# Attention scores in PSUM: four banks in turn for the exponentials, three for the maxima, with their products issued singly

## The chip, the cores and the metric

The kernel runs on one core of a Trainium2 chip. The metric is the device time of one execution in microseconds; lower is better. The kernel before has a median of 2086.16 us over three runs (2078.07 to 2087.5). TensorE (PE) multiplies and writes PSUM, VectorE (DVE) and ScalarE (ACT) read PSUM, GpSimd (POOL) works on SBUF, SyncE (SP) issues transfers.

## What is computed

One hybrid block in fp32 on x of shape (4, 1024, 256): attention, a routed feed-forward layer, a Mamba-2 layer, and the same feed-forward layer again, each on a layer norm of x and added to x. Only the attention is touched:

```python
Q, K, V = (split(Q), split(K), split(V))      # 16 heads of 16, from multi-LoRA projections
Q, K = (_rope(Q), _rope(K))
scores = jnp.einsum('bhqd,bhkd->bhqk', Q, K) / jnp.sqrt(jnp.asarray(D_KV, x.dtype))
causal = jnp.tril(jnp.ones((s, s), bool))
scores = jnp.where(causal, scores, jnp.asarray(-jnp.inf, scores.dtype))
attn = jax.nn.softmax(scores, axis=-1)
out = jnp.einsum('bhqk,bhkd->bhqd', attn, V)
out = out.transpose(0, 2, 1, 3).reshape(b, s, D_MODEL)
return _multilora(out, ids, Wo, Ao, Bo)
```

## The kernel before

The scores are computed twice. A first pass only finds the largest score of each row of Q. A second pass computes the scores transposed, with that maximum already subtracted inside the product (an extra row of operands), so that ACT can take the exponential straight from PSUM.

The work is cut into 16 units (`UNITS`: 4 batches by 4 groups of 4 heads). A unit has 24 steps (`CORE`), 384 in all, and two pairs of heads, which alternate. TensorE's program is one list, in this order at each step:

- `shifted(U, n)` (L940 to L951): the second pass. Two products, one for each head of the pair, on rows 0 to 63 and rows 64 to 127 of the array, of 512, 384, 256 or 128 columns. They go to two banks of `a_ps_e`, which has `HEAD_BANKS` banks used in turn. Ahead of the first of the two stands the one wait for both banks: on the semaphore `exp_done` of ACT's exponentials (L947).
- `scores(k)` (L928 to L938): the first pass. Products, called chunks, are numbered k from 0 to 767 (`TOTAL`), and come in pairs k and k+1, again one for each half of the array. On average there is one pair per step, but the table `CUTS` gives some steps none and others two. Each chunk takes a bank of `a_ps_m`.
- pieces: LoRA weights ("lora"), transposes of x ("xt"), projections of Q and K ("qk"), of V ("v") and of the output ("out"), and the transpose of the row maxima ("max"). Each takes one bank of `a_ps_m` as well.
- `weigh_at(N - 4)` (L973): the exponentials of an earlier step times V, into `a_ps_a`.

Chunks and pieces together make one list, `entries`, and entry i uses bank i mod `BANKS` of `a_ps_m`. `bank_of` (L848) waits until entry i minus `BANKS` (`BEFORE`) has been read out: a chunk by its maximum on DVE (`chunk_max`), a "lora" or "out" piece by DVE, the other pieces by ACT. PSUM has 8 banks: `HEAD_BANKS` is 3, `BANKS` is 4, and `a_ps_a` has one.

On the other side, `exponential` (L767) runs two ACT instructions per step (L774), one for each bank of the pair. `maxima` (L505) runs one DVE instruction per chunk: on a chunk that crosses the diagonal, an add of the causal mask with a running maximum (L511, followed by a read of the accumulator), on the others a plain reduction (L515). Between them DVE does layer norms, merges and row statistics. All engines run their own instructions strictly in program order, so a wait at `scores(k)` on TensorE also holds back everything behind it in the list: the weighing, the next `shifted`, and with that ACT.

Of the kernel before, what the change touches and what calls it, by code (L numbers as in the profile page):

```python
# [22 lines left out]
P = 128  # L23
# [90 lines left out]
def attention(nc, X, C, A):  # L114
# [2 lines left out]
    UNITS = BATCH * GROUPS  # L117
    BUFS = 5
    RING = 7
    BANKS = 4  # L120
    HEAD_BANKS = 3
    STEPS = [(c, j) for c in range(2) for j in range(HALF * (c + 1))]
    NS = len(STEPS)
    CORE = 2 * NS
# [11 lines left out]
    def width(k):  # L136
        i, c, _ = CHUNKS[k % NC]
        return min(512, (i + 1) * P - 512 * c)
# [60 lines left out]
    entries += LATE  # L199
    BANK = {e: i % BANKS for i, e in enumerate(entries)}  # L200
    BY_DVE = [e for e in entries if e[0] in ("lora", "out")]
# [7 lines left out]
    SELECT_NO = {e: i for i, e in enumerate(SELECTS)}  # L209
    BEFORE = {e: entries[i - BANKS] for i, e in enumerate(entries) if i >= BANKS}  # L210
    assert len(BANK) == len(entries)

    with ExitStack() as held, ExitStack() as ctx:
        sems = Semaphores(nc, held)

        def sb(name, shape, dt=F32):
            return ctx.enter_context(nc.sbuf_tensor("a_" + name, shape, dt))
# [3 lines left out]

        ps_e = ctx.enter_context(nc.psum_tensor("a_ps_e", [P, HEAD_BANKS, 512], F32))
        ps_m = ctx.enter_context(nc.psum_tensor("a_ps_m", [P, BANKS, 512], F32))
        ps_a = ctx.enter_context(nc.psum_tensor("a_ps_a", [P, 512], F32))
# [31 lines left out]
        q_st = sb("q_st", [P, BUFS, SEQ], F32R)  # L256
# [39 lines left out]
        def rows(r):  # L296
            return slice(64 * r, 64 * r + 64)
# [428 lines left out]
        def _(act):  # L726
# [40 lines left out]
            def exponential(U, n):  # L767
# [4 lines left out]
                for r in range(2):  # L772
                    act.wait_ge(shifted_ps, 2 * N + r + 1)
                    nc.scalar.activation(probs[:, N % RING, r, q0:], ps_e[:, (2 * N + r) % HEAD_BANKS, q0:], ACT.Exp,  # L774
                                         scale=DH ** -0.5).then_inc(exp_done, 1)
# [11 lines left out]
            for m in range(4):  # L787
                act.wait_ge(wt_ps, m + 1)
                nc.scalar.copy(w_t[:, m], ps_e[:, m % HEAD_BANKS, :].rearrange("p (t d) -> p t d", t=DT)).then_inc(wt_sb, 1)
            act.dma_start(rope[:], A["rope"]).then_inc(rope_in, 16)  # L790
            for m in range(4):
                act.wait_ge(wt_ps, 5 + m)
                nc.scalar.copy(b_t[:, m], ps_e[0:64, (4 + m) % HEAD_BANKS, 0:D]).then_inc(wt_sb, 1)
            for e in EARLY:
# [34 lines left out]
        def _(pe):  # L829
            ident = C["ident"]  # L830
            pe.wait_ge(w_in, 16 * 4)
            for m in range(4):
                if m >= HEAD_BANKS:
                    pe.wait_ge(wt_sb, m - HEAD_BANKS + 1)
                for d in range(DT):
# [12 lines left out]
            def bank_of(e):  # L848

                if e in BEFORE:  # L850
                    old = BEFORE[e]
                    if old[0] == "chunk":
                        pe.wait_ge(chunk_max, old[1] + 1)
                    elif old in ACT_NO:
                        pe.wait_ge(piece_act, ACT_NO[old] + 1)
                    else:
                        pe.wait_ge(piece_dve, DVE_NO[old] + 1)
                return ps_m[:, BANK[e]]
# [69 lines left out]
            def scores(k):  # L928

                p, (i, c, _) = k // NC, CHUNKS[k % NC]  # L930
                banks = [bank_of(("chunk", k + r)) for r in range(2)]
                if k % NC == 0:
                    pe.wait_ge(pair_in[p % BUFS], 32 * (p // BUFS + 1))
                w = width(k)
                for r in range(2):
                    nc.tensor.matmul(banks[r][:, 0:w], q_st[rows(r), p % BUFS, i * P:(i + 1) * P],  # L936
                                     k_st[rows(r), p % BUFS, 512 * c:512 * c + w], start=True, stop=True
                                     ).then_inc(score_ps, 1)  # L938

# [53 lines left out]
            for k in range(0, CUTS[0], 2):  # L993
                scores(k)
                if k + 1 in AMID:
                    piece(AMID[k + 1])
            for U in range(UNITS):
                for n in range(CORE):
                    N = U * CORE + n
                    shifted(U, n)  # L1000
                    for k in range(issued_after(N - 1), issued_after(N), 2):
                        scores(k)
                    for e in pieces_after(U, n):
                        piece(e)
                    if N >= 4:
                        weigh_at(N - 4)
                    if N >= 2 and issued_after(N - 2) == TOTAL:
                        keep_warm()
# [1336 lines left out]
def phase_attention(nc, X, C, I, out):  # L2345
    A = {k: I["L0_attn_a_" + k] for k in ("Wq", "Wk", "Wv", "Wo", "Aq", "Ak", "Av", "Ao", "Bq", "Bk", "Bv", "Bo")}
    A["x"] = I["L0_attn_a_x"].rearrange("b (t p) d -> p (b t) d", p=P)
    A["Wd"] = I["L0_ffn_Wd"]
    A["starts"], A["rope"] = I["L0_attn_a_lora_start_indices"], I["const_rope"]
    attention(nc, X, C, A)  # L2350
# [33 lines left out]
```

## Time and profile before

| | us |
|---|---|
| median of three runs | 2086.16 |
| lowest and highest run | 2078.07, 2087.5 |
| the profiled execution | 2072.31 |
| its span, first to last instruction | 2070.6 |
| PE busy | 1789.2 (86%) |
| DVE busy | 1274.9 (62%) |
| ACT busy | 866.1 (42%) |
| mean granted TensorE clock | 0.915 of full speed |

The profile is of one execution. 1.7 us of it lie outside the span. The stage with both passes of the scores runs from 118 us, where the first `shifted` stands, to 744 us; before it, from 60 to 118 us, TensorE runs the first chunks alone. After 744 us come the feed-forward and Mamba stages, which have their own PSUM tiles. Busy time of PE is not time at its peak: matmuls are pipelined, and their ends are modelled. A row of the timeline merges neighbours of one kind: "x2" is the pair for two heads.

### The profile page before, as it was taken

The page shows a single profiled execution, that of the slowest core. Times are in us where ns is not written, and L with a number is a line of the kernel's source. Part 1 is how long each engine was busy: PE and PEld are TensorE (multiplying, and loading weights), DVE is VectorE, ACT ScalarE, POOL GpSimd, SP SyncE. Part 2 cuts the span into 40 slices and gives each one's busy share as a digit, 9 for nine tenths or more (in the row PEclk, how much of TensorE's full clock was granted, in tenths as well). Part 3 has the DMA queues.
Part 4 walks back from the last instruction along what each step waited for, and adds up shares of the span by engine and source line. Part 5 has one row for each costly group of instructions (what it writes and reads, how often), then busy time and mean ns, then how long its engine had stood idle before and what let it go on. Part 6 is the DMA issues. An engine that isn't in the chain of part 4 may idle for free. (4 is left out here: it accounts for less than half of the span.)

```text
span 2070.6 us, 32175 instructions
## 1 busy us (share of the span) xinstructions
PE 1789.2 (86%) x10573; PEld 1197.9 (58%) x10573; DVE 1274.9 (62%) x3120; ACT 866.1 (42%) x1791; POOL 717.5 (35%) x873
## 2 busy tenths in 40 slices
PE   5578988989988874999999488989898957999998
PEld 4234443444434332888888346657483836888886
DVE  4487677677678318555555366665666666555554
ACT  2146666665666633222222155554546451222221
POOL 2326446445364421223232223422342312222231
PEclk8679999989989886999999789998999978999999
DMA  5624344343455524576776520201102044676764
GB/s 153 210 82 132 103 139 139 110 145 117 122 164 168 178 88 189 200 254 247 249 254 234 181 92 1 103 1 40 64 1 103 1 184 177 238 256 241 256 246 172
DMA packets 103470, 312.37 MB, mean 151 GB/s; under 512 B 23304, under 2 KB 54796, under 8 KB 93200
## 3 DMA queue, kind: packets, MB, share of 16 engines
q1 hardware_dynamic: 86016, 257.08, 35.4%
q0 software_dynamic: 15936, 50.35, 8.0%
q10 hardware_dynamic: 1360, 2.89, 0.4%
q8 instruction: 92, 1.51, 0.3%
q14 instruction: 66, 0.54, 0.1%
HBM read 245.12 MB, written 53.87 MB: 144 GB/s over the span
## 5 line engine op out<-in xcount | busy, mean ns | idle before, releaser
L774 ACT ACTIVATE a_probs<-a_ps_e 128x512 f32<-128x512 f32 (+3 forms) x768 | 336.2, 491 | 153.1 <-PE a_ps_e L949 149.3
L511 DVE CUSTOM_DVE_ANT_0 a_ps_m<-a_ps_m,a_causal 128x512 f32<-128x512 f32 (+3 forms) x512 | 238.1, 517 | 79.8 <-PE a_ps_m L936 79.0
L1460 ACT CAST hidden_high<-g_ps_h 128x512 fp32r<-128x512 f32 x140 | 75.2, 590 | 398.9 <-PE g_ps_h L1605 398.9
L515 DVE TENSOR_REDUCE a_peak<-a_ps_m 128x1 f32<-128x512 f32 x256 | 164.1, 683 | 94.4 <-PE a_ps_m L936 93.3
L949 PE MATMUL a_ps_e<-a_q_st,a_k_st 64*128 64x512 f32 (+3 forms) x768 | 179.4, 461 | 32.8 <-ACT a_probs L774 22.5
L966 PE MATMUL a_ps_a<-a_probs,a_vals 128*32 128x256 f32 (+2 forms) x2560 | 201.3, 388 | 0.0
L936 PE MATMUL a_ps_m<-a_k_st,a_q_st 64*128 64x512 f32 (+3 forms) x768 | 154.1, 399 | 51.1 <-DMA a_k_st<-a_scr_k 23.0
L653 POOL TENSOR_SCALAR_AFFINE_SELECT a_probs<-a_probs 128x256 f32<-128x256 f32 x256 | 104.0, 408 | 260.1 <-ACT a_probs L774 258.7
L111 POOL TENSOR_TENSOR g_xe_rs<-g_xe_ve,table 128x1 f32<-128x1 f32 x70 | 39.3, 561 | 441.8 <-DVE g_xe_ve L1301 441.7
L949 PEld LDWEIGHTS a_ps_e<-a_q_st,a_k_st 64*128 64x128 f32 x768 | 75.6, 192 | 191.4 <-ACT a_probs L774 136.0
L1593 PE MATMUL g_ps_y<-g_w_d,hidden_high 128*128 128x512 f32 x560 | 144.4, 400 | 5.9 <-DVE x_res L1337 5.9
L1455 ACT ACTIVATE x_res<-g_ps_g 128x1024 f32<-128x1024 f32 x70 | 71.9, 1028 | 171.4 <-PE g_ps_g L1578 117.4
L936 PEld LDWEIGHTS a_ps_m<-a_k_st,a_q_st 64*128 64x128 f32 x768 | 83.9, 204 | 86.7 <-issue 36.1
L1321 DVE TENSOR_TENSOR x_res<-x_res,g_ps_u 128x1024 f32<-128x1024 f32 x70 | 85.5, 1221 | 69.1 <-PE g_ps_u L1578 69.1
L1593 PEld LDWEIGHTS g_ps_y<-g_w_d,hidden_high 128*128 128x128 f32 x560 | 106.4, 190 | 32.0 <-issue 6.3
L1328 DVE TENSOR_TENSOR hidden_less<-g_ps_h,hidden_high 128x512 fp32r<-128x512 f32 x140 | 90.2, 687 | 47.5 <-ACT hidden_high L1460 47.5
L1374 POOL DMA_INDIRECT x_res<-g_x_rows,g_token_i x70 | 75.8, 1083 | 93.6 <-DVE g_token_i L1274 73.1
L1313 DVE CAST g_xe_hi<-g_ps_x 128x256 fp32r<-128x256 f32 x70 | 29.7, 425 | 121.0 <-PE g_ps_x L1538 120.9
L1971 POOL TENSOR_TENSOR m_y<-m_y,m_z_act 128x512 f32<-128x512 f32 x32 | 40.6, 1269 | 162.5 <-DVE m_y L1879 162.5
L966 PEld LDWEIGHTS a_ps_a<-a_probs,a_vals 128*32 128x32 f32 x2560 | 51.7, 110 | 74.1 <-issue 49.2
L1578 PE MATMUL g_ps_g<-g_w_hi,g_xe_hi 128*128 x272 | 91.4, 417 | 0.3 <-DVE g_xe_hi L1313 0.3
L1578 PE MATMUL g_ps_u<-g_w_hi,g_xe_hi 128*128 x272 | 85.8, 397 | 0.0
(298 smaller groups left out, 3871.5 us busy)
## 6 DMA issues: line engine op xcount, KB each, us to landing
g_w_d<-down_rows SPq DMA_DIRECT2D x70, 2048.0 KB, 7.8
a_q_st<-a_scr_q POOLq DMA_DIRECT2D x32, 512.0 KB, 4.2
a_k_st<-a_scr_k POOLq DMA_DIRECT2D x32, 512.0 KB, 5.5
m_spread_acs<-m_acs_rows SPq DMA_DIRECT2D x8, 2048.0 KB, 9.7
a_scr_q<-a_high SPq DMA_DIRECT2D x34, 256.0 KB
a_scr_k<-a_high SPq DMA_DIRECT2D x32, 256.0 KB
a_swapped<-a_raw SPq DMA_DIRECT2D x64, 128.0 KB, 2.0
g_x_rows<-x_res SPq DMA_DIRECT2D x8, 1024.0 KB, 12.5
```

The costliest lines, as they stand in the source:

```text
L511: nc.vector.tensor_tensor_reduce(ps_m[:, bank, 0:w], ps_m[:, bank, 0:w], causal[:, 512 - w:], 1.0, MASKED, ALU.add, ALU.max, peak[:, p % 2 ...
L515: nc.vector.tensor_reduce(peak[:, p % 2, r, i, c:c + 1], ps_m[:, bank, 0:w], AX, ALU.max).then_inc(chunk_max, 1)
L653: nc.gpsimd.affine_select(tile, tile, [[0, 2], [1, P]], ALU.is_ge, 0.0, base=0, channel_multiplier=-1).then_inc(masked, 1)
L774: nc.scalar.activation(probs[:, N % RING, r, q0:], ps_e[:, (2 * N + r) % HEAD_BANKS, q0:], ACT.Exp, scale=DH ** -0.5).then_inc(exp_done, 1)
L936: nc.tensor.matmul(banks[r][:, 0:w], q_st[rows(r), p % BUFS, i * P:(i + 1) * P], k_st[rows(r), p % BUFS, 512 * c:512 * c + w], start=True, ...
L949: nc.tensor.matmul(ps_e[:, (2 * N + r) % HEAD_BANKS, q0:], k_st[rows(r), p % BUFS, j * P:(j + 1) * P], q_st[rows(r), p % BUFS, 512 * c + q ...
L966: last = nc.tensor.matmul(ps_a[32 * u:32 * u + 32, some], vals[:, b % 2, j, 17 * h:17 * h + 32], probs[:, (U * CORE + 2 * m + u // 2) % RI ...
L1321: nc.vector.tensor_tensor(hid, gate, ps_u[:].rearrange("p b f -> p (b f)"), ALU.mult).then_inc(hid_ready, 1)
L1328: nc.vector.tensor_tensor(hid_lo[:, some], ps_h[:, c], hid_hi[:, some].bitcast(F32), ALU.subtract).then_inc(ht_lo, 1)
L1374: nc.gpsimd.indirect_dma_start(out=xe[:, j % XE], out_offset=None, in_=x_rows, in_offset=bass.IndirectOffsetOnAxis(ap=token_i[:, j:j + 1], ...
L1578: last = nc.tensor.matmul(ps[:, c], x[:, d * P:(d + 1) * P], w[:, :, d].rearrange("p a f -> p (a f)"), start=(n == d == 0), stop=(n == len ...
L1593: nc.tensor.matmul(ps_y[:], hid_hi[:, f * P:(f + 1) * P], w[:, f], start=(f == 0), stop=False, skip_group_check=True)
```

## The change

Two constants change, and `scores` asks for a bank immediately ahead of each product and not for both ahead of the first:

```diff
-    BANKS = 4
-    HEAD_BANKS = 3
+    BANKS = 3
+    HEAD_BANKS = 4
...
             def scores(k):
 
                 p, (i, c, _) = k // NC, CHUNKS[k % NC]
-                banks = [bank_of(("chunk", k + r)) for r in range(2)]
                 if k % NC == 0:
                     pe.wait_ge(pair_in[p % BUFS], 32 * (p // BUFS + 1))
                 w = width(k)
                 for r in range(2):
-                    nc.tensor.matmul(banks[r][:, 0:w], q_st[rows(r), p % BUFS, i * P:(i + 1) * P],
+                    bank = bank_of(("chunk", k + r))
+                    nc.tensor.matmul(bank[:, 0:w], q_st[rows(r), p % BUFS, i * P:(i + 1) * P],
                                      k_st[rows(r), p % BUFS, 512 * c:512 * c + w], start=True, stop=True
                                      ).then_inc(score_ps, 1)
```

No instruction is added, removed or put elsewhere; what differs is what each waits for. In numbers of the two lists:

| | before | now |
|---|---|---|
| first `shifted` product of step N waits for exponential | 2N-2 (first of step N-1) | 2N-3 (second of step N-2) |
| chunk k (even) waits for the maximum of chunk | k-4 and k-3 | k-3 |
| chunk k+1 waits for the maximum of chunk | nothing further | k-2 |
| a piece, or a chunk behind pieces, waits for the entry | 4 places back | 3 places back |

(The rows for chunks hold where the entries in between are chunks too.)

The order of TensorE's instructions shows the new wait. This is a place in the score stage at which two pairs of chunks stand in a row (512 and 384 columns), before; L949 is `shifted`, L936 is `scores`, L966 the weighing, L884 a "qk" piece:

```order
L949 MATMUL a_ps_e<-a_q_st,a_k_st 128x512 [waits a_exp_done]
L949 MATMUL a_ps_e<-a_q_st,a_k_st 128x512
L936 MATMUL a_ps_m<-a_k_st,a_q_st 128x512 [waits a_chunk_max,a_piece_act]
L936 MATMUL a_ps_m<-a_k_st,a_q_st 128x512
L936 MATMUL a_ps_m<-a_k_st,a_q_st 128x384 [waits a_piece_act,a_chunk_max]
L936 MATMUL a_ps_m<-a_k_st,a_q_st 128x384
L966 MATMUL a_ps_a<-a_probs,a_vals 32x128 [waits a_masked,a_exp_done]
```

The same kind of place on TensorE in the changed kernel, a little earlier in the list, with no piece three entries back:

```order
L949 MATMUL a_ps_e<-a_q_st,a_k_st 128x512 [waits a_exp_done]
L949 MATMUL a_ps_e<-a_q_st,a_k_st 128x512
L936 MATMUL a_ps_m<-a_k_st,a_q_st 128x512 [waits a_chunk_max] x2
L936 MATMUL a_ps_m<-a_k_st,a_q_st 128x384 [waits a_chunk_max] x2
L966 MATMUL a_ps_a<-a_probs,a_vals 32x256 [waits a_masked,a_exp_done]
```

The second product of each pair has got a wait of its own ("x2" with a wait is two instructions, each with its wait). `shifted` keeps one wait for both of its products; only the number it waits for is one lower.

## Rows read from the trace of the kernel before

**Rows 1.** Busy time by stretch: length, then us of each engine (instructions), PEclk

```profile
60.00:118.00 58.00, 31.67 (x76) 13.07 (x78) 36.15 (x113) 7.28 (x14) 27.82 (x28) 0.56 0.60 199
118.00:744.00 626.00, 564.23 (x4483) 258.46 (x4481) 429.97 (x1369) 400.32 (x918) 298.66 (x450) 0.94 0.43 130
...
744.00:2070.00 1326.00, 1161.16 (x5912) 903.96 (x5912) 784.92 (x1577) 446.36 (x839) 376.49 (x380) 0.93 0.44 159
```

**Rows 2.** Waits from 118 to 744 us: total, times, longest

```profile
ACT a_probs L774 <- PE a_ps_e L949: 149.3, 271, 3.0
PEld a_ps_e L949 <- ACT a_probs L774: 136.0, 257, 2.4
...
PE a_ps_e L949 <- ACT a_probs L774: 22.5, 58, 2.0
```

**Rows 3.** The line of `scores` from 118 to 744 us: what it waited for

```profile
  DVE a_peak L511: 31.9, 68
...
  DVE a_peak L515: 6.4, 20
```

**Rows 4.** The same view of L936: who waited for it (us, times)

```profile
  DVE a_peak L515: 71.7, 65
  DVE a_ps_m L511: 70.6, 60
```

**Rows 5.** Timeline of PE, 256.5 to 262.2 us: start, us, instruction, [idle before]

```profile
256.64 0.64 PE L966 MATMUL a_ps_a<-a_probs,a_vals 128*32 128x256 f32 x8
257.23 0.50 PE L949 MATMUL a_ps_e<-a_q_st,a_k_st 64*128 64x512 f32 x2
257.56 0.22 PE L936 MATMUL a_ps_m<-a_k_st,a_q_st 64*128 64x128 f32 x2
257.72 0.64 PE L966 MATMUL a_ps_a<-a_probs,a_vals 128*32 128x256 f32 x8
258.47 0.50 PE L949 MATMUL a_ps_e<-a_q_st,a_k_st 64*128 64x512 f32 x2
258.81 0.57 PE L936 MATMUL a_ps_m<-a_k_st,a_q_st 64*128 64x512 f32 x4
259.30 0.64 PE L966 MATMUL a_ps_a<-a_probs,a_vals 128*32 128x256 f32 x8
259.96 0.49 PE L949 MATMUL a_ps_e<-a_q_st,a_k_st 64*128 64x512 f32 x2
260.79 0.39 PE L936 MATMUL a_ps_m<-a_k_st,a_q_st 64*128 64x256 f32 x2 [0.33 <-DVE a_peak L511]
261.10 0.64 PE L966 MATMUL a_ps_a<-a_probs,a_vals 128*32 128x256 f32 x8
261.67 0.50 PE L949 MATMUL a_ps_e<-a_q_st,a_k_st 64*128 64x512 f32 x2
```

**Rows 6.** Timeline of DVE in the same stretch

```profile
259.24 0.70 DVE L511 CUSTOM_DVE_ANT_0 a_ps_m<-a_ps_m,a_causal 128x512 f32<-128x512 f32 x1 [0.68 <-PE a_ps_m L936]
259.85 0.14 DVE L511 DVE_READ_ACCUMULATOR2_ANT a_peak<- 128x1 f32 x1
...
260.50 0.14 DVE L511 DVE_READ_ACCUMULATOR2_ANT a_peak<- 128x1 f32 x1
...
261.02 0.14 DVE L511 DVE_READ_ACCUMULATOR2_ANT a_peak<- 128x1 f32 x1
```

**Rows 7.** Timeline of ACT in the same stretch

```profile
257.82 1.09 ACT L774 ACTIVATE a_probs<-a_ps_e 128x512 f32<-128x512 f32 x2 [0.15 <-PE a_ps_e L949]
...
259.30 1.10 ACT L774 ACTIVATE a_probs<-a_ps_e 128x512 f32<-128x512 f32 x2
```

**Rows 8.** Timeline of PE: first and last `shifted` behind an exponential, last pair of chunks

```profile
121.91 0.68 PE L949 MATMUL a_ps_e<-a_q_st,a_k_st 64*128 64x384 f32 x1
...
702.62 0.22 PE L936 MATMUL a_ps_m<-a_k_st,a_q_st 64*128 64x128 f32 x2
...
726.68 0.50 PE L949 MATMUL a_ps_e<-a_q_st,a_k_st 64*128 64x512 f32 x2 [0.53 <-ACT a_probs L774]
```

**Rows 9.** Timelines of PE and DVE: the first late pair, the first and last late piece

```profile
118.53 0.45 PE L936 MATMUL a_ps_m<-a_k_st,a_q_st 64*128 64x256 f32 x2
118.34 1.29 DVE L515 TENSOR_REDUCE a_peak<-a_ps_m 128x1 f32<-128x512 f32 x2 [0.43 <-PE a_ps_m L936]
126.22 1.21 PE L866 MATMUL a_ps_m<-a_b_t,a_low_and_less 64*128 64x256 f32 x2
...
666.06 0.28 PE L912 MATMUL a_ps_m<-table,a_less 128*16 128x128 f32 x1
```

## The prediction

> **What bounds the kernel now.** I read the busy time by stretch first. The change can only act between 60 and 744 us, where the attention runs, and above all from 118 to 744 us, where both passes of the scores do. In those 626 us PE is busy for 564.2 us, DVE for 430.0 and ACT for 400.3 [rows 1]. PE is the bound, and every microsecond for which its in-order list stands still is nearly lost; DVE and ACT have room on average. The 1326 us behind it are not touched.
>
> The waits come next. Exponentials and their products wait for each other: ACT stands idle 149.3 us (271 times) until `shifted` has delivered, and PE's loads of `shifted` stand 136.0 us (257 times), its matmuls 22.5 us (58 times), until ACT has freed a bank [rows 2]. That is a ring, and the change widens it. For `scores`, PE stands 31.9 and 6.4 us (88 times) until DVE has taken a maximum [rows 3], while DVE waits for a chunk only 65 + 60 = 125 times for the 712 chunks of the stage [rows 4]. At the other 587 the chunk lay ready when DVE came to it: the maxima mostly run behind, on the cushion of four banks, which the change cuts to three.
>
> **The first part: four banks for the exponentials.** `shifted` of step N need no longer wait for the first exponential of step N-1. What that wait costs PE is not the 136 us, since the array is still draining earlier matmuls during most of it. I price it from starts. With nothing to wait for, `shifted` begins 261.67 - 261.10 = 0.57 us behind the start of the weighing ahead of it. At 257.23 it took 0.59, at 258.47 0.75, at 259.96 0.66 us [rows 5]. The second of these is tied to ACT: its exponentials start at 257.82 and take 1.09 us for two, so the first ends about 258.4, and `shifted` starts 0.05 us behind it [rows 7]. So three steps lose 0.02, 0.18 and 0.09 us. In the stage, 177 `shifted` start within 0.15 us of the exponential that frees them, the first at 121.91 and the last at 726.68, where PE stood fully idle for 0.53 us [rows 8]. At 0.1 us each that is 18 us, at 0.2 us 35 us; the low end that the waits give outright is 22.5 us, the high end 136.0 + 22.5 = 158.5 us [rows 2], which counts the draining too. I take 0.17 us x 177 = 30 us, between the small losses of a plain step and the long ones like 0.53 us. All of it goes, because the exponential now waited for is an exponential (0.55 us) earlier.
>
> What is late next: PE. ACT, at 400 of 626 us, follows easily. The weighing needs exponentials of three steps back or more and gains no wait.
>
> **The second part: three banks for the maxima.** The even chunk waits for k-3 as before, since the old pair waited for both k-4 and k-3. The new wait is the odd chunk's, on k-2, and that of pieces on the entry three back. The stretch that I read shows what it does. At 258.81 us PE issues four chunks in a row (512, 512, 384, 384 columns, call them a, b, c, d) [rows 5]. DVE finishes a at 259.85 + 0.14 = 259.99, b at 260.64, c at 261.16 [rows 6]. Now d needs the bank of a. A chunk starts 0.15 us behind the maximum that frees it (260.64, then 260.79), so d starts at 260.14 and no longer beside c, ahead of 259.30. Behind d stands the weighing. It follows a pair of 128 columns by 0.16 us (257.56, 257.72) and one of 256 by 0.31 (260.79, 261.10); with 0.26 us it starts at 260.40 where it was 259.30. Then comes `shifted` (0.57 later, 260.97 for 259.96), then the next pair (0.34 later, 261.31 for 260.79). PE was 1.1 us late, and 0.33 us of standing and the wait for ACT, which stood there anyway, give part of it back: 0.52 us remain. Queued behind d are the weighing and, for ACT, the next `shifted`.
>
> Next the number of such places. I held each start on PE against the end of the maximum (or the evacuation) that would now be waited for. From 118 us on, 149 of 355 pairs start earlier than the maximum that their second product would need has ended, from 118.53 (DVE takes two reductions from 118.34 to 119.63, and the first of them frees that bank near 119.0) [rows 9] to 702.62 [rows 8], in sum 67.8 us. Of the pieces 52 of 106 do, from 126.22 to 666.06 [rows 9], in sum 23.4 us. Together 91 us, the high end if nothing of it were given back. The low end is 0: while DVE runs at full rate PE's delay is only taken from a later wait on DVE. Going through the stage place by place as in the worked one (a delay is carried on, shrinks by each standstill that PE had anyway, and counts when DVE next runs dry), about 38 us remain over 71 places, 0.54 us each, which agrees with the 0.52 us worked out above. I take 38 us.
>
> Here the Trainium skill bears on issuing singly. The trace shows two pairs of 512 and 384 columns issued in 0.57 us, "x4" in one row, so the halves of the array work side by side [rows 5]. The page "TensorE: Matmul & The Clock Gate", section "Part 3: Packing small matmuls — row/col tiling", says that matmuls on different row groups overlap with starts some 4 ns apart, and that the load of weights for another row group is pulled ahead of matmuls in flight. By that rule a wait already met costs nothing; whether a wait on the second load hinders the pulling ahead, no page says and no row here shows.
>
> For that I bound it: below at 0, above at half of a pair lost where the wait is already met. Two chunk pairs start at 258.81 and leave to the weighing at 259.30, so 0.49 us for two pairs, 0.25 for one [rows 5]; half, 0.12 us, for the 355 - 149 = 206 pairs in time makes 25 us. I take 0, since the two products have separate weights and rows, and keep 25 us for the range.
>
> **How the parts meet.** They aren't independent. Where `shifted` no longer waits, PE comes to the next chunk earlier, and in places where DVE is behind it waits there instead. 149 of 355 pairs (42%) are such places, so 0.42 x 30 = 12 us of the first gain come back as wait on DVE. The sum is -30 + 12 + 38 = +20 us. From 60 to 118 us the chunks are bound by DVE and by transfers; DVE with three banks always has a chunk waiting, so I put that stretch at 0, and the start, where transposes of weights use four banks for three, at 0 as well (PE waits for transfers there).
>
> The profiled execution took 2072.31 us, its span 2070.6: the sum made against it gives 2092 us. The median of the runs shown is 13.9 us above it, 2086.16; I forecast on that, 2086 + 20 = 2106 us.
>
> **Rivals.** First, the ring of exponentials is worth more than the cushion (faster). The trace speaks for it with 149.3 us of idle ACT and 158.5 us of PE and its loads at that wait [rows 2]; if PE really lost 0.3 us at each of the 177 places (53 us), and the maxima gave back more than half of their delay (25 us left, 10 more for the interplay), the sum is -53 + 25 + 10 = -18, and the time 2068 us. It decides if DVE catches up between bunches of chunks; the 587 chunks that lay waiting speak against. Second, they cancel: 30 won, 12 returned, 20 lost by the banks, 2088 us. This is so if most of the late pairs merely move a wait that PE had anyway. Third, the serialised pairs: 25 us on top of the forecast and the pieces' 23.4 us in full instead of in part (some 10 more), 2141 us. What speaks for it is that the halves now run side by side in every pair [rows 5]; what speaks against is that nothing but a met wait stands between them. Fourth, the change does nothing because the shared bound is elsewhere: PE's own work at 564 of 626 us [rows 1] would be that, and it gives 2086 us; it falls together with the second.
>
> The clock is a risk, not a rival: it was 0.94 in the stage and 0.56 in the one before it, where PE was busy for 31.67 of 58 us [rows 1]. More standing on PE could bring more of the lower level (1.2 GHz) into the stage; that lies inside the upper end.
>
> **How the numbers follow.** Forecast (1% slower or so): 0.46. Serialised or otherwise worse: 0.12. Cancelling: 0.20. Faster: 0.22. The range goes from 2066, just under the time of the faster case, to 2138, just under the serialised one with all its terms. The forecast's own range is 2096 to 2125. A measurement of this kernel can tell some 0.5% (10 us) from no change. Faster by over 0.5%: 0.22; within 0.5%: 0.20; slower by over 0.5%: 0.58.
>
> **What would show it.** In the changed profile PE's waits of `shifted` on ACT fall from 257 and 58 times to a few dozen. PE's waits of `scores` on DVE rise from 38 us to some 80, most of them at the second product. DVE's waits for chunks rise from 142 us as PE's do, since the stage gets longer: it ends near 764 us. The behaviour after that stage is unchanged at 1326 us. The row of four chunks merged at 258.81 falls apart into single ones. I am wrong if the stage is shorter than 626 us, if waits on ACT stay (then the ring was not of banks), or if pairs with their wait met start over 0.05 us apart (then it is the third case).

## The result and the profile after

| | before | changed |
|---|---|---|
| median, us (4 runs each) | 2083.7 | 2103.8 |
| lowest and highest | 2078.07, 2087.5 | 2099.37, 2113.6 |
| ratio, 95% interval | | 1.0092 (1.0064 to 1.012) |
| profiled execution, us | 2072.31 | 2104.42 |

The change makes the kernel 20 us slower (13 to 25 by the interval of the ratio); 2106 us was forecast. The profiled executions lie 32 us apart, since the one of before, at 2072.31 us, took 11 us less than its median. Four executions that stood apart from the others of their kernel (5694.2 us of `change_in_pairs`; 2894.2, 2104.1 and 2108.1 us of the kernel before, beside the experiments) are left out of all ratios and medians below.

Busy time by stretch for the changed kernel (length, then PE, PEld, DVE, ACT, POOL, granted clock, DMA share, GB/s), the stretches of [rows 1], the second one up to the end of the stage, which is now at 778 us:

```profile
60.00:118.00 58.00, 44.86 (x83) 20.44 (x83) 34.63 (x113) 7.27 (x14) 27.88 (x28) 0.59 0.60 199
118.00:778.00 660.00, 604.57 (x4479) 287.83 (x4482) 431.65 (x1371) 394.09 (x917) 296.89 (x450) 0.91 0.40 123
778.00:2102.00 1324.00, 1160.24 (x5924) 904.42 (x5916) 786.70 (x1577) 446.30 (x839) 374.55 (x380) 0.93 0.44 159
```

The difference is in one place. The score stage takes 660 us where it took 626; what stands ahead of it is equal, and the rest takes 1324 for 1326 us. DVE and ACT do the same work in it, 432 and 394 us, and are idle for the rest. The mean granted clock of the stage reads 0.91 where it read 0.94.

`single_only`, described below, serves as a second profile of the kernel before: it differs only in asking for each bank singly, with no measurable difference in time (its profiled execution took 2082.27 us, near the median of before). Its stage:

```profile
118.00:754.00 636.00, 580.31 (x4478) 269.90 (x4477) 427.97 (x1368) 399.12 (x917) 298.19 (x450) 0.91 0.42 127
```

Against it the stage grew by 24 us, at the same clock of 0.91. So some 10 of the 34 us between the two profiled stages come from the choice of the execution and not from the change.

What the line of `scores` waited for from 118 to 778 us, and who waited for it, beside [rows 3, 4]:

```profile
  DVE a_peak L511: 63.2, 126
  DVE a_peak L515: 45.3, 87
...
who waited for it (us, times):
  DVE a_peak L515: 86.3, 85
  DVE a_ps_m L511: 84.3, 85
```

PE's waits on maxima grew from 38.3 us (88 times) to 108.5 us (213 times), and DVE's own waits for chunks from 142.3 to 170.6 us. Both sides wait more: that is what a shorter queue between two engines does.

The line of `shifted` in the same stretch, beside [rows 2]:

```profile
  issue: 78.1, 185
  ACT a_probs L774: 66.9, 167
  DMA a_q_st<-a_low_and_less: 1.8, 2
who waited for it (us, times):
  ACT a_probs L774: 172.1, 223
```

The waits on ACT fell from 136.0 + 22.5 = 158.5 us (315 times) to 66.9 us (167 times), and even the rest is hardly a wait for ACT. This view puts a gap down to the exponential that ended in it, whichever it was. Held against the one exponential that the program waits for, 180 of 382 first products of `shifted` start within 0.15 us of its end before, and 3 of 382 now; half of them now start over 1.5 us behind it. The ring was widened, as meant, and no longer binds. ACT nevertheless stands idle for longer, 172.1 us for 149.3 (156.9 in `single_only`), now because PE comes late.

The place that the forecast worked through, a, b, c and d, lies here in the changed kernel. Timeline of PE:

```profile
268.55 0.50 PE L949 MATMUL a_ps_e<-a_q_st,a_k_st 64*128 64x512 f32 x2
268.89 0.57 PE L936 MATMUL a_ps_m<-a_k_st,a_q_st 64*128 64x512 f32 x3
270.13 0.44 PE L936 MATMUL a_ps_m<-a_k_st,a_q_st 64*128 64x384 f32 x1 [0.68 <-DVE a_peak L511]
270.50 0.64 PE L966 MATMUL a_ps_a<-a_probs,a_vals 128*32 128x256 f32 x8
271.07 0.50 PE L949 MATMUL a_ps_e<-a_q_st,a_k_st 64*128 64x512 f32 x2
271.41 0.28 PE L936 MATMUL a_ps_m<-a_k_st,a_q_st 64*128 64x256 f32 x2
```

DVE at the same place, the maximum of a and the read that ends it:

```profile
269.32 0.70 DVE L511 CUSTOM_DVE_ANT_0 a_ps_m<-a_ps_m,a_causal 128x512 f32<-128x512 f32 x1 [0.54 <-PE a_ps_m L936]
269.94 0.14 DVE L511 DVE_READ_ACCUMULATOR2_ANT a_peak<- 128x1 f32 x1
```

And ACT behind it:

```profile
269.53 1.10 ACT L774 ACTIVATE a_probs<-a_ps_e 128x512 f32<-128x512 f32 x2
271.66 1.09 ACT L774 ACTIVATE a_probs<-a_ps_e 128x512 f32<-128x512 f32 x2 [1.04 <-PE a_ps_e L949]
```

The row of four products has become three and one. The fourth waits until the maximum of the first is read at 270.08 and starts at 270.13. From a to the next pair it is 271.41 - 268.89 = 2.52 us, where it was 260.79 - 258.81 = 1.98 us for the same chunks [rows 5]: 0.54 us lost, 0.52 forecast. ACT then stands for 1.04 us, for a product queued behind d.

### The profile page after: what moved, and what is told of

Same layout as the page of the kernel before. It is cut to its first block and busy times, and to the rows that moved or that the text cites. A ratio compares the mean times of both kernels' runs of the same rounds, so it can differ in the third digit from the quotient of the medians.

```text
span 2102.7 us, 31824 instructions
## 1 busy us (share of the span) xinstructions
PE 1839.5 (87%) x10573; PEld 1233.3 (59%) x10573; DVE 1276.7 (61%) x3120; ACT 859.8 (41%) x1791; POOL 714.0 (34%) x873
## 5 line engine op out<-in xcount | busy, mean ns | idle before, releaser
L774 ACT ACTIVATE a_probs<-a_ps_e 128x512 f32<-128x512 f32 (+3 forms) x768 | 330.8, 496 | 173.1 <-PE a_ps_e L949 172.1
L511 DVE CUSTOM_DVE_ANT_0 a_ps_m<-a_ps_m,a_causal 128x512 f32<-128x512 f32 (+3 forms) x512 | 239.3, 515 | 95.1 <-PE a_ps_m L936 94.9
L936 PE MATMUL a_ps_m<-a_k_st,a_q_st 64*128 64x512 f32 (+3 forms) x768 | 208.8, 411 | 55.1 <-DVE a_peak L511 20.6
L515 DVE TENSOR_REDUCE a_peak<-a_ps_m 128x1 f32<-128x512 f32 x256 | 164.0, 682 | 108.9 <-PE a_ps_m L936 108.3
L966 PE MATMUL a_ps_a<-a_probs,a_vals 128*32 128x256 f32 (+2 forms) x2560 | 209.4, 402 | 0.0
L936 PEld LDWEIGHTS a_ps_m<-a_k_st,a_q_st 64*128 64x128 f32 x768 | 119.1, 207 | 116.7 <-DVE a_peak L511 51.3
L949 PE MATMUL a_ps_e<-a_q_st,a_k_st 64*128 64x512 f32 (+3 forms) x768 | 185.4, 462 | 0.8 <-DMA a_q_st<-a_low_and_less 0.8
L949 PEld LDWEIGHTS a_ps_e<-a_q_st,a_k_st 64*128 64x128 f32 x768 | 80.0, 196 | 146.5 <-issue 78.1
L1455 ACT ACTIVATE x_res<-g_ps_g 128x1024 f32<-128x1024 f32 x70 | 71.9, 1027 | 171.3 <-PE g_ps_g L1578 117.2
L966 PEld LDWEIGHTS a_ps_a<-a_probs,a_vals 128*32 128x32 f32 x2560 | 52.5, 112 | 74.1 <-issue 51.8
L1578 PE MATMUL g_ps_u<-g_w_gu,g_xe_hi 128*128 x272 | 85.8, 397 | 0.0
```

Of the source, the lines that this page charges most:

```text
L511: nc.vector.tensor_tensor_reduce(ps_m[:, bank, 0:w], ps_m[:, bank, 0:w], causal[:, 512 - w:], 1.0, MASKED, ALU.add, ALU.max, peak[:, p % 2 ...
L515: nc.vector.tensor_reduce(peak[:, p % 2, r, i, c:c + 1], ps_m[:, bank, 0:w], AX, ALU.max).then_inc(chunk_max, 1)
L936: nc.tensor.matmul(bank[:, 0:w], q_st[rows(r), p % BUFS, i * P:(i + 1) * P], k_st[rows(r), p % BUFS, 512 * c:512 * c + w], start=True, sto ...
L949: nc.tensor.matmul(ps_e[:, (2 * N + r) % HEAD_BANKS, q0:], k_st[rows(r), p % BUFS, j * P:(j + 1) * P], q_st[rows(r), p % BUFS, 512 * c + q ...
L966: last = nc.tensor.matmul(ps_a[32 * u:32 * u + 32, some], vals[:, b % 2, j, 17 * h:17 * h + 32], probs[:, (U * CORE + 2 * m + u // 2) % RI ...
L1578: last = nc.tensor.matmul(ps[:, c], x[:, d * P:(d + 1) * P], w[:, :, d].rearrange("p a f -> p (a f)"), start=(n == d == 0), stop=(n == len ...
```

## The experiments

Numbers of runs differ (4 to 12 of each kernel, 13 to 35 of before), and the groups were measured on different chips with a kernel before of their own (medians 2084.1, 2087.3 and 2085.3 us). So differences between two kernels are taken from their ratios, with an interval worked out from both, and 1% is 21 us.

**First group: one constant or one line at a time.**

`cushion_only` is the changed kernel with the ring as it was:

```diff
-    HEAD_BANKS = 4
+    HEAD_BANKS = 3
```

> The changed kernel with HEAD_BANKS back at 3: three banks for the maxima and single issue, but the ring of the exponentials as before (7 banks of 8 in use). Theory (the prediction's sum): the cushion alone costs 38 us and the ring is worth 30 less 12 given back, so this is 38 us slower than before (ratio 1.018) and some 18 us slower than the changed kernel. Rival (the ring is worth nothing, all of the change's loss is the cushion's): within 5 us of the changed kernel, ratio 1.009.

Measured: 2123.7 us, ratio 1.0196 (1.0144 to 1.0247). The cushion alone costs some 41 us (30 to 51), and the fourth bank of the ring brings 22 of them back (10 to 34; 20 by medians). This agrees with the forecast's sum, term by term: 38, and 30 - 12 = 18. The rival falls.

`single_only` is the kernel before with the new `scores` and the old banks:

```diff
-                banks = [bank_of(("chunk", k + r)) for r in range(2)]
...
                 for r in range(2):
...
+                    bank = bank_of(("chunk", k + r))
```

> Before, with single issue alone: BANKS 4, HEAD_BANKS 3, each chunk asks for its bank right ahead of its product. Theory: a wait that is already met does not keep the halves of the array apart, and the second product waits for the maximum that the pair waited for already, so the ratio is 1.000, within 0.3%; starts of the two products stay some 3 ns apart where the wait is met. Rival (serialised pairs): slower by up to 25 us, ratio 1.012, with starts over 50 ns apart everywhere.

Measured: 2081.6 us, ratio 0.9984 (0.9953 to 1.0016), no difference. In its trace 267 of the 354 pairs of the stage start within 20 ns of each other, where 340 of 355 did before. The others are no sign of serialising: where the bank of the second product was free when the first started, 221 of 240 pairs are within 20 ns and 6 over 50 ns apart; where it was not, none of 55 is within 20 ns. (Pairs that wait for a piece are not in these two counts.) In those 55 the first product starts early and the second waits for the maximum that both waited for. The serialised pairs are ruled out.

`change_in_pairs` has the changed banks with the `scores` of before:

> The changed banks (3 for the maxima, 4 for the exponentials) with the pair waits of before: both banks asked for ahead of the first product. Theory: the first product then waits for the maximum k-2 too, TensorE stands the same time and does less in it: slower than the changed kernel by 106 split pairs at up to 0.2 us of product that now stands behind the wait, 10 to 20 us, ratio to before 1.014 to 1.019. Rival (single issue brings nothing): equal to the changed kernel, 1.009.

Measured: 2141.0 us in three executions, ratio 1.0287 (1.0213 to 1.0362), a miss in size: single issue is worth 41 us at three banks (24 to 57; 37 by medians), not 10 to 20. What its line of `scores` waited for, in the whole execution, then who waited for it:

```profile
  DVE a_peak L511: 115.9, 146
  DVE a_peak L515: 87.1, 117
...
who waited for it (us, times):
  DVE a_peak L515: 115.1, 91
  DVE a_ps_m L511: 102.5, 99
```

In the changed kernel the same view has 71.9 + 55.2 = 127.1 us for PE and 108.3 + 94.9 = 203.2 us for DVE; here PE has 203.0 and DVE 217.6. I had counted only the product that moves behind the wait. A pair that needs two of three banks can be issued only when a single chunk is left for DVE, so both products come late, and DVE runs dry more. The trace adds a second part: a pair that waits starts 0.14 to 0.15 us behind the maximum (184 pairs here), where a product that waits alone starts 0.05 us behind it (the median of 131 in the changed kernel). Some 208 pairs here start within 0.26 us behind their maximum, so that is an estimated 208 x 0.09 = 19 us. No run tests the two parts apart.

`narrow_ring` shifts the other way, with the `scores` of before:

```diff
-    BANKS = 4
-    HEAD_BANKS = 3
+    BANKS = 5
+    HEAD_BANKS = 2
```

> The opposite shift: BANKS 5, HEAD_BANKS 2, pair waits. shifted of step N waits for both exponentials of step N-1. Theory: the ring is worth about 0.2 us at a place now and a whole exponential (0.55 us) at most steps when one more bank goes: 384 steps at 0.3 to 0.5 us, less 20 us that a fifth bank for the maxima gives back: 95 to 170 us slower, ratio 1.045 to 1.08. Rival (the cushion of the maxima is what counts): at most 1.01.

Measured: 2157.2 us, ratio 1.0378 (1.0322 to 1.0435), 79 us slower (67 to 91): the ring counts, but somewhat less than the low end of 95. The line of `shifted` waited in it for:

```profile
  ACT a_probs L774: 323.6, 442
  issue: 57.5, 98
```

That is twice the 158.5 us of [rows 2]. From 5 and 2 over 4 and 3 to 3 and 4 banks the ratio goes 1.0378, 1, 1.0287 with pair waits; with single issue it is 0.9984 and 1.0092 for the last two. Four and three is the best of the three splits, in either way of issuing where both were tried.

**Second group: the same with light maxima**, so that DVE is less often behind. Each maximum reads half of its chunk and leaves out the rest, and the mask:

```diff
-                    bank, w = BANK["chunk", k], width(k)
+                    bank, w = BANK["chunk", k], width(k) // 2
...
-                        nc.vector.tensor_tensor_reduce(ps_m[:, bank, 0:w], ps_m[:, bank, 0:w], causal[:, 512 - w:], 1.0,
+                        nc.vector.tensor_tensor_reduce(ps_m[:, bank, 0:w], ps_m[:, bank, 0:w], causal[:, 0:w], 1.0,
```

> The kernel before with lighter maxima: each DVE maximum reads only the first half of its chunk's columns, without the causal mask, so that part of the maxima is left out. DVE's maxima shrink from some 383 us to about 250, and DVE is never behind. Theory: TensorE's waits on DVE (38 us at scores) vanish, 15 to 30 us faster than before, ratio 0.986 to 0.993; the ring of the exponentials stays, with its some 140 us of load waits on ACT. Rival (waits on DVE cost nothing, as TensorE drains meanwhile): 1.000.

> The changed kernel with the same lighter maxima (first half of the columns, no mask: that part of the maxima is left out). With DVE never behind, three banks should do as well as four, and only the ring's gain is left. Theory: 20 to 40 us faster than the same kernel with the banks of before (light_before), so some 45 to 65 us faster than the full kernel before, ratio 0.97 to 0.98. Rival (the ring is worth only what the two bank counts showed, about 20 us at best, and the short bank chain of pieces still costs): within 10 us of light_before.

Measured: `light_before` 2056.9 us, ratio 0.9857 (0.9819 to 0.9894); `light_changed` 2063.0 us, 0.9869 (0.9842 to 0.9896). The first is 30 us faster than before, at the far edge of what was expected; its line of `scores` still waits for DVE, 23.1 us in the whole execution for 70.8, and DVE waits for a chunk 268 times for 130, at the first chunk of a pair (there are 384 pairs). The second does not agree: no gain of the ring is left over, and the number is the rival's. Either the ring is worth nothing once DVE is quick, or the cushion still costs as much as the ring gives. `light_cushion`, with `HEAD_BANKS = 3` again, tells these apart:

> Three banks for the maxima, single issue, HEAD_BANKS 3, with lighter maxima (each reads only the first half of its chunk's columns, no mask: that part of the maxima is left out). Beside light_before (4 and 3 banks, 2056.9 us) and light_changed (3 and 4 banks, 2063.0 us) it splits their difference of 6 us. Theory: the ring is worth 20 us or more with any bank count, and the cushion still costs that much with light maxima, since chunks come in bunches of two pairs: 2080 to 2095 us. Rival: with light maxima neither the ring nor the cushion is worth anything: 2055 to 2068 us.

Measured: 2087.7 us, ratio 1.0012 (0.9986 to 1.0038). So with light maxima the cushion costs 32 us (23 to 42) and the ring gives 30 us (22 to 38) back; by medians, which lie in two groups, 31 and 25. My picture of the cushion had been wrong in one point: I thought it needed DVE to be behind. The trace of `light_cushion` shows 49 pairs of the stage whose products start over 0.15 us apart, and 45 of them are second pairs directly behind another, each of which waits. Where four products come in one burst, a DVE that reads half the columns cannot free a bank in time either.

**Third group: taking the bursts apart.** `spread_changed` puts the weighing between the pairs of a burst:

```diff
-                    for k in range(issued_after(N - 1), issued_after(N), 2):
+                    ks = list(range(issued_after(N - 1), issued_after(N), 2))
+                    for k in ks[:1]:
                         scores(k)
+                    if len(ks) > 1 and N >= 4:
+                        weigh_at(N - 4)
+                    for k in ks[1:]:
+                        scores(k)
                     for e in pieces_after(U, n):
                         piece(e)
-                    if N >= 4:
+                    if len(ks) < 2 and N >= 4:
                         weigh_at(N - 4)
```

> The changed kernel with the weighing put between the first pair of chunks and the rest at steps with two or more pairs, nothing else. Theory: the loss of three banks sits at two pairs in a row (the fourth product waits for the first maximum), so here most of it goes: 12 to 25 us faster than the changed kernel, ratio to before 0.997 to 1.003. Rival: the cushion is lost at single pairs too, where DVE is behind anyway: within 8 us of the changed kernel, ratio 1.005 to 1.01.

Measured: 2094.3 us, ratio 1.0036 (1.0003 to 1.0068), some 12 us better than the changed kernel (3 to 21), between what theory and rival said. That is about half of the net loss, and a quarter or so of the 41 us that the cushion costs. In the changed kernel 106 of 355 pairs start over 0.15 us apart, 73.4 us in sum: all 45 second pairs of a burst, 33.3 us, and 61 others, 40.1 us. With the bursts taken apart there are still 116 such pairs, 63.9 us in sum: the late products have become shorter in sum rather than fewer, so a good part of the cushion's cost lies outside the bursts.

`exps_single` applies single issue to `shifted`, with the banks of before:

```diff
-                if N >= 1:
-                    pe.wait_ge(exp_done, max(2 * N + 2 - HEAD_BANKS, 1))
                 for r in range(2):
+                    if 2 * N + r >= HEAD_BANKS:
+                        pe.wait_ge(exp_done, 2 * N + r + 1 - HEAD_BANKS)
```

> Before (4 and 3 banks, pair waits for chunks), with the two products of shifted issued singly: the first waits for exponential 2N-3, the second for 2N-2. Nothing is left out. Theory: the release of the second is when the pair was released before, but ACT gets the first half of its pair earlier, so its idle 149 us shrink and the ring turns faster: 5 to 25 us faster, ratio 0.988 to 0.998. Rival: TensorE stands at the second product as long as at the pair, and issues them one behind the other instead of side by side: 0 to 20 us slower, 1.00 to 1.01.

Measured: 2079.3 us, ratio 0.9964 (0.9934 to 0.9994), a small gain, at the low end of theory. The view of `shifted` has 94.6 us (215 times) of waits on ACT over the whole execution, where it had 158.5 us (315 times). That looks like most of what a fourth bank does, but the wait has only moved: 155 second products now start within 0.15 us of the exponential that frees their bank (and 13 first ones), where a fourth bank leaves 3 first ones. What was expected of ACT did not come either: it is idle for 160.5 us before its exponentials, no less than 149.3 before or 158.1 in `single_only`.

`both_single` joins it with the single issue of chunks, and `spread_before` adds the spreading of bursts, both with 4 and 3 banks:

> Banks as before (4 and 3), single issue for the chunks and for shifted, nothing left out. Theory: the two are independent, 0.9984 and 0.9964, so 0.995, 10 us faster than before. Rival: what single issue of the chunks gives is spent by the other: 0.997 or more.

> As both_single, and at steps with two or more pairs of chunks the weighing is put between the first pair and the rest. Theory: the chunk that waits for DVE gets 0.5 us more, so that waits on DVE (some 40 us) shrink by a third to a half: 5 to 15 us faster than both_single, ratio to before 0.988 to 0.993. Rival: the wait only moves to the next shifted: equal to both_single.

Measured: 0.9973 (0.9948 to 0.9998) and 0.9947 (0.9921 to 0.9973), 2075.5 and 2072.5 us. `both_single` is nearer to its rival, but its interval holds both. `spread_before` is 3 us better than that by medians, 5 by ratios (-2 to 13; 5 to 15 were expected), so the gain of spreading is not shown; its waits of `scores` on DVE did not shrink as expected but went from 38.5 to 47.1 us. It is the fastest kernel here that leaves nothing out: 0.5% faster than before. That bursts matter less where there are four banks to take them is likely, but not shown.

## Why the prediction was right, point by point

- **The sum, -30 + 12 + 38 = +20 us.** Measured +20 us by medians. The pair of terms that can be measured apart, the cushion alone and then the ring on top, came to 41 (30 to 51) and -22 (-34 to -10), for 38 and -18. The mechanism and both sizes are confirmed within these intervals; that the sum fits to the microsecond is luck.
- **The ring's 30 us with four banks for the maxima** could not be measured: that needs nine banks. With three banks for the maxima it is worth 22 us with full and 30 us with light maxima. But the last of the 16 units has no chunks, so there the ring stands alone. The window from its first `shifted` to its last, before and then in the changed kernel, both at full clock:

```profile
711.40:741.80 30.40, 28.94 (x224) 11.56 (x223) 0.35 (x1) 21.26 (x48) 6.36 (x17) 1.00 0.29 89
747.60:776.30 28.70, 28.70 (x224) 11.55 (x223) 0.35 (x1) 20.73 (x48) 6.14 (x16) 1.00 0.30 94
```

  `cushion_only`, with three banks for the ring, has 30.4 us there as well. 1.7 us in each of 16 units would be 27 us, an estimate that fits the 30. That 12 of 30 are given back in the units with chunks is a split that no run shows; only the difference is confirmed.
- **"The maxima mostly run behind":** overstated. Of the 587 chunks that lay ready, more than half were second chunks of a pair, which are always ready, because the two products start together (3 ns apart in the median): all 125 waits of [rows 4] stand before first chunks. Of some 356 pairs 125 found DVE waiting and 231 did not. The light kernels show what hangs on it: with DVE waiting twice as often, three quarters of the cushion's cost remain (32 of 41 us). So the 38 us came out right with a cause that was only in part the one given.
- **0.52 us at the worked place:** 0.54 us. One detail was off: a product that waits alone starts 0.05 us behind its maximum (270.08, then 270.13), not 0.15; in return the weighing starts 0.37 us behind it for the 0.26 assumed.
- **The count of late places:** 149 pairs were held to be late by 67.8 us in sum; in the changed kernel 138 are over 20 ns apart, 75.3 us in sum (106 of them over 0.15 us, 73.4 us). Slightly fewer and later ones.
- **A wait that is met costs nothing** (taken as 0, bounded at 25 us): right, by `single_only`. This also shows what was left open there: a met wait at the second product did not keep the halves apart. In the changed kernel itself, where the second product's bank was free in time, 202 of 216 pairs are within 20 ns, and 7 over the 50 ns that would have spoken for the serialised pairs.
- **Waits of `shifted` on ACT "to a few dozen":** not by the view that was named, which still has 167 of loads, 66.9 us. Counted against the exponential that is really waited for, nearly all went (180 before, close to the 177 of the forecast, and 3 now), and "all of it goes" was right. The sign chosen was the weak part, since that view does not know which exponential a product needs.
- **Waits of `scores` "some 80 us":** 108.5 us in the stage, more by a third. "Most at the second product" holds for PE's matmuls: 73 of their 76 waits on DVE.
- **The stage "ends near 764 us":** it ended near 778. The 20 us were added to a profile that was itself some 10 us shorter in this stage than another of a kernel of the same speed, `single_only`. The next part separates this.

**How much of it was the clock.** A unit of the stage can be compared where the granted clock was full in both. Windows of units 2, 3, 7 and 11 before (the first unit is 0), from the first `shifted` of each to that of the next:

```profile
196.80:233.10 36.30, 33.92 (x296) 17.07 (x292) 26.76 (x86) 24.88 (x57) 16.76 (x29) 1.00 0.47 142
233.10:270.20 37.10, 33.84 (x278) 13.95 (x274) 26.09 (x86) 25.81 (x59) 26.32 (x37) 1.00 0.38 120
392.20:429.40 37.20, 33.98 (x278) 13.94 (x274) 26.05 (x86) 25.91 (x59) 26.29 (x37) 1.00 0.39 119
557.80:594.30 36.50, 33.64 (x280) 13.84 (x276) 26.03 (x86) 25.80 (x59) 24.32 (x33) 1.00 0.38 120
```

The same units of `single_only`, whose stage took 10 us longer:

```profile
199.00:235.00 36.00, 34.18 (x296) 17.57 (x292) 26.61 (x86) 24.80 (x57) 16.75 (x29) 1.00 0.48 144
235.00:272.50 37.50, 34.66 (x280) 14.46 (x276) 25.89 (x86) 25.61 (x59) 26.00 (x36) 1.00 0.39 119
402.60:440.10 37.50, 34.40 (x280) 14.38 (x276) 25.92 (x86) 25.83 (x59) 26.48 (x37) 1.00 0.40 121
566.50:602.70 36.20, 33.89 (x280) 14.13 (x276) 25.82 (x86) 25.72 (x59) 24.28 (x33) 1.00 0.40 121
```

And of the changed kernel:

```profile
204.40:242.50 38.10, 35.24 (x295) 18.56 (x292) 27.08 (x86) 24.48 (x57) 16.68 (x29) 1.00 0.44 136
242.50:280.40 37.90, 35.19 (x280) 15.52 (x276) 26.23 (x86) 25.31 (x59) 25.83 (x35) 1.00 0.39 117
414.50:452.40 37.90, 35.19 (x280) 15.55 (x276) 26.24 (x86) 25.41 (x59) 25.84 (x35) 1.00 0.39 117
584.40:622.30 37.90, 35.20 (x278) 15.53 (x274) 26.24 (x86) 25.28 (x59) 24.14 (x32) 1.00 0.38 117
```

The four units take 147.1 us before, 147.2 in `single_only` and 151.8 in the changed kernel. At full clock the change costs 1.17 us per unit, which would be 19 us for 16: about all of the 20 us by medians. The 10 us between the stages of the first two lie in the other units, where the clock was lower (0.91 for 0.94 over the stage). So most of what goes beyond 20 us in the 34 is the clock of the one execution profiled before, and not the change. Whether the change adds a little by way of the clock is not shown.

## What to carry to other kernels

When PSUM banks are shared between two loops, price both queues: here the queue that lost a bank cost 41 us, and the ring that got it gained 22. With a quicker consumer the two were nearly even (32 and 30), so the consumer's lag alone does not decide. Look at bursts first: every one of the 45 places with two pairs in a row got a late product here, and an in-order engine then holds back work that has nothing to do with the bank. Ask for each bank right ahead of its product: that costs nothing where the wait is met and is worth more where there are fewer banks (nothing measurable at four, 41 us at three). When a change is meant to end a wait, count the starts tied to the very event that is waited for, and not only the waits that a view puts down to an engine. And compare two profiles of the same kernel before reading 10 us from one.

## What the runs showed of the hardware

Two products on different halves of the TensorE array start within 20 ns of each other in most cases also when each has a semaphore wait of its own, if it is already met (221 of 240 such pairs of `single_only`, 202 of 216 of the changed kernel). If it is not, the second starts 0.05 us behind the end of the DVE instruction that frees its bank (median of 131 in the changed kernel); a pair that waits ahead of its first product starts 0.14 to 0.15 us behind it (184 of the pairs of `change_in_pairs`).

The granted clock was lower where the stage got much longer. From 118 us to the stage's end it was 0.94 before (626 us) and 0.91 in the changed kernel (660 us); in `cushion_only`, in `change_in_pairs` and in `narrow_ring`, in this order:

```profile
118.00:797.00 679.00, 616.94 (x4474) 289.33 (x4477) 435.11 (x1375) 400.68 (x918) 297.12 (x449) 0.89 0.39 120
```

```profile
118.00:810.00 692.00, 607.47 (x4482) 279.24 (x4482) 445.20 (x1382) 396.19 (x918) 297.48 (x451) 0.88 0.38 118
```

```profile
118.00:827.00 709.00, 605.73 (x4465) 270.88 (x4469) 433.35 (x1363) 402.46 (x915) 296.67 (x448) 0.85 0.37 114
```

Means like these lie between the levels of 2.4 and 1.2 GHz. They do not follow the length of the stage where it changes little: `single_only` had 0.91 in 636 us and `spread_before` 0.90 in 632 us, no more than the changed kernel in 660. Over whole executions, `narrow_ring` (0.890 to 0.893 in four) and `change_in_pairs` (0.898 to 0.903 in three) lie below all 13 of the kernel before beside them (0.904 to 0.922), and `cushion_only` (0.901 to 0.914) does not. So only for those two is it more than the scatter between executions. What the clock alone is worth was not tried.
